# Attention and feed-forward layer on one core: the values matmuls of each step in two halves of 256 queries, with the step loops written out

## What is computed

```python
xn = _layernorm(x)
# attention: 32 query heads of 16, 8 key/value heads, 1024 tokens; bitnet_linear is a matmul with
# the signs of the weights and one factor per output
q, k, v = bitnet_linear(xn, wq, sq), bitnet_linear(xn, wk, sk), bitnet_linear(xn, wv, sv)
scores = jnp.einsum('bhqd,bhkd->bhqk', q, k) / np.sqrt(16)
attn = jax.nn.softmax(scores, axis=-1)
out = jnp.einsum('bhqk,bhkd->bhqd', attn, v)
# feed-forward, 512 -> 1792 -> 512
hidden = _silu(xn @ gate_w.T) * (xn @ up_w.T)
x = x + bitnet_linear(out, wo, so) + hidden @ down_w.T
```

## Time and profile before

| | |
|---|---|
| three runs | 572.05, 576.71, 576.72 us, median 576.71 |
| the profiled execution | 578.11 us |
| its span, first to last instruction | 576.4 us (1.7 us lie around it) |
| PE busy | 513.6 us, 89% |
| DVE busy | 451.4 us, 78% |
| ACT busy | 341.8 us, 59% |
| mean granted TensorE clock | 0.978 |

### The profile page before, as it was taken

One profiled execution on the slowest core, in us unless ns is written; L12 is line 12 of the kernel. 1 busy time (PEld: TensorE's weight loads), 2 busy tenths in 40 slices (PEclk: granted clock), 3 DMA queues, 4 the chain that ended last, 5 costly groups with the idle time before them and its releaser, 6 DMA issues.

```text
span 576.4 us, 9428 instructions
## 1 busy us (share of the span) xinstructions
PE 513.6 (89%) x3001; PEld 162.2 (28%) x3001; DVE 451.4 (78%) x534; ACT 341.8 (59%) x620; POOL 91.0 (16%) x112
## 2 busy tenths in 40 slices
PE   1598977699997999997999997999999998999995
PEld 0354433233332222221222221222222222222442
DVE  6949848776775899997999997999999962221797
ACT  1563324223235788886888886888888875666000
POOL 4503243333323000000000000000001011051021
PEclk9999999899998899998999998999999998999999
DMA  8612654422104421101102102101111003352311
GB/s 251 164 30 63 144 88 92 117 39 37 20 1 58 73 54 37 52 22 36 46 27 54 34 19 56 35 19 54 35 53 58 20 11 89 79 150 66 101 73 55
DMA packets 29949, 36.19 MB, mean 63 GB/s; under 512 B 6544, under 2 KB 20752, under 8 KB 29912
## 3 DMA queue, kind: packets, MB, share of 16 engines
q1 hardware_dynamic: 20600, 24.19, 14.2%
q0 software_dynamic: 8304, 10.95, 10.2%
q10 hardware_dynamic: 1008, 0.61, 0.5%
HBM read 30.62 MB, written 10.35 MB: 71 GB/s over the span
## 4 chain that ended last, share of the span: by engine, by line
PE 71%; DVE 13%; ACT 6%; issue 5%; DMA 2%; ACTq 1%; POOL 0%; SPq 0%; DVEq 0%; POOLq 0%
PE ps L1147 21%; PE ps L1117 16%; PE ps L1033 14%; PE ps L1085 8%; PE ps L1042 7%; ACT room L635 5%; DVE nmx L769 2%; PE ps L1171 2%; PE ps L1014 2%; DVE room L706 1%; DMA ga<-r_scratch 1%; DMA hlo<-x 1%; DVE ga L762 1%; DVE y L765 1%; ACTq L631 1%
## 5 line engine op out<-in xcount | busy, mean ns | idle before, releaser
L769 DVE TENSOR_REDUCE nmx<-ps 128x1 f32<-128x1024 f32 x256 | 302.2, 1219 | 19.1 <-PE ps L1042 14.4
L635 ACT ACTIVATE room<-ps 128x512 f32<-128x512 f32 x512 | 266.3, 604 | 72.3 <-PE ps L1117 67.6
L1117 PE MATMUL ps<-qst,kB 50*128 50x512 f16 x512 | 156.9, 391 | 24.0 <-ACT room L635 16.1
L1042 PE MATMUL ps<-kA,qst 48*128 48x512 f16 x512 | 161.9, 392 | 3.4 <-DVE nmx L769 3.3
L1147 PE MATMUL ps<-room,vcur 128*32 128x512 f32 x1024 | 140.6, 622 | 0.5 <-ACT room L635 0.5
L1033 PE MATMUL ps<-room,wf 128*128 128x512 f16 x448 | 105.2, 390 | 8.3 <-DVE room L864 7.2
L1117 PEld LDWEIGHTS ps<-qst,kB 50*128 50x128 f16 x512 | 37.5, 94 | 178.9 <-ACT room L635 142.2
L1033 PEld LDWEIGHTS ps<-room,wf 128*128 128x128 f16 x448 | 43.3, 100 | 67.6 <-issue 22.4
L616 ACT ACTIVATE room<-ps,gsc 128x512 f32<-128x512 f32 x28 | 19.2, 686 | 68.6 <-PE ps L1033 68.6
L1042 PEld LDWEIGHTS ps<-kA,qst 48*128 48x128 f16 x512 | 35.1, 94 | 43.5 <-DVE nmx L769 35.0
L496 POOL TENSOR_TENSOR hlo<-room,hhi 128x512 f16<-128x512 f32 x28 | 33.5, 1196 | 82.3 <-ACT hhi L573 72.9
(11 more groups left out here) (126 smaller groups left out, 292.9 us busy)
## 6 DMA issues: line engine op xcount, KB each, us to landing
qst<-q_scratch SPq DMA_DIRECT2D x32, 192.0 KB, 3.3
o_scratch<-osb SPq DMA_DIRECT2D x16, 256.0 KB, 2.1
q_scratch<-parts SPq DMA_DIRECT2D x12, 256.0 KB
hlo<-x SPq DMA_DIRECT2D x8, 256.0 KB, 6.8
parts<-x POOLq DMA_DIRECT2D x8, 256.0 KB, 3.2
wf<-gate POOLq DMA_DIRECT2D x14, 128.0 KB, 3.1
wf<-up POOLq DMA_DIRECT2D x14, 128.0 KB, 3.2
wd<-down POOLq DMA_DIRECT2D x1, 1792.0 KB, 13.4
```

Source lines behind the costliest of these rows:

```text
L635: nc.scalar.activation(probs[:, s % 2, r, :], ps[:, score_bank(entry(j, i)), :], ACT.Exp, scale=gam_reg[r]).then_inc(scores_free, 1)
L769: nc.vector.tensor_reduce(nmx[:, hf, idx:idx + 1], bank_pair(idx % 2), AX.X, ALU.max, negate=True).then_inc(rows_free, 1)
L1042: return nc.tensor.matmul(ps[:, 2 * (idx % 2) + b, :], qst[low:low + KROWS, par, hf, head, qt * P:(qt + 1) * P], kA[low:low + KROWS, par, ...
L1117: nc.tensor.matmul(ps[:, score_bank(e), :], kB[low:low + SROWS, par, kt % (TT // 2) * P:(kt % (TT // 2) + 1) * P], qst[low:low + SROWS, pa ...
```

## The change

- The `Fori` loops of all five engines become Python loops: every step is written out.
- `times_values` is issued in two parts of 256 queries: part 0 behind the second score, part 1 behind the fourth. Each has its own four matmuls.
- The four row matmuls of a step follow the first, the second and, two of them, the third score. None follows the fourth.
- `split_max` leaves DVE. ACT copies the transposed maxima to a new tile `mxs` (`take_max`), and POOL makes the two parts from it. PE waits for ACT's copy (`max_taken`) only. POOL's copy of the next group's values (`next_values`) is put between these. `normalize_io(pool, 0)` goes ahead of the last of them.
- ACT loads the next group's factors one in each of the last four steps of a group, into a second set of registers.

```diff
-            def split_max(v, hf, first=False):
-
-                maxT = ps[0:UNITS, 6 if first else score_bank(T_ENTRY), 0:P]
-                dve.wait_ge(maxT_ready, v + 1)
-                nc.vector.tensor_scalar(shp[:, hf, 0, :], maxT, 1.0 / LIFT, None, ALU.mult).then_inc(shift_step, 1)
...
+            def take_max(v, bank):
+
+                act.wait_ge(maxT_ready, v + 1)
+                act.wait_ge(shift_ready, v)
+                nc.scalar.activation(mxs[:, :], ps[0:UNITS, bank, 0:P], ACT.Copy, scale=1.0 / LIFT).then_inc(max_taken, 1)
...
+            def split_max(v, hf):
+
+                pool.wait_ge(max_taken, v + 1)
+                nc.gpsimd.tensor_tensor(shp[:, hf, 0, :], mxs[:, :], ones[0:UNITS, :], ALU.mult).then_inc(shift_step, 1)
+                pool.wait_ge(shift_step, v + 1)
+                nc.gpsimd.tensor_tensor(shp[:, hf, 1, :], mxs[:, :], shp[:, hf, 0, :], ALU.subtract).then_inc(shift_ready, 1)
...
-            with act.Fori(0, NP - 1) as gp:
+            for gp in range(NP - 1):
...
-            def exps(gp, s):
+            def exps(gp, s, last):
...
-                if j == 0 and hf == 0:
-                    for r in range(REP):
-                        act.reg_load(gam_reg[r], gam_words[0:1, bass.ds(gp_ * (2 * REP) + par * REP + r, 1)])
+                if j == T_STEP + 1 and not (last and s >= STEPS + TT):
+                    take_max(gp * 4 + s // TT + 1, score_bank(T_ENTRY))
...
+                if hf == 1 and j >= TT - REP and not (last and par == 1):
+                    load_scale(gp_ * 2 + par + 1, 1 - par, j - (TT - REP))
...
                     if e - 3 == T_ENTRY and transposes:
-                        pe.wait_ge(shift_ready, block_ + 2)
+                        pe.wait_ge(max_taken, block_ + 2)
...
-                    if with_rows:
-                        idx = 2 * j + i // 2
-                        n = (gp_ * 2 + par + 1) * (2 * UNITS) + hf * UNITS + idx
+                    idx = 2 * j + i // 2
+                    if with_rows and i < REP - 1:
                         if i % 2 == 0:
-                            pe.wait_ge(rows_free, n + 1)
+                            pe.wait_ge(rows_free, (gp_ * 2 + par + 1) * (2 * UNITS) + hf * UNITS + idx + 1)
                         mm = half_rows(1 - par, hf, idx, 1 - half)
                         if i % 2 == 1:
                             mm.then_inc(rows_ready, 1)
-                    elif i == 0:
+                        if i == REP - 2:
+                            half_rows(1 - par, hf, idx, half).then_inc(rows_ready, 1)
+                    elif not with_rows and i == 0:
                         for n in fill:
                             down_proj(*FILLS[n])
-                    if i == REP - 1 and not opening:
-                        times_values(gp, s - 1)
+                    if i % 2 == 1 and not opening:
+                        times_values(gp, s - 1, i // 2)
...
+                of = slice(part * (HALF // 2), (part + 1) * (HALF // 2))
                 for r in range(REP):
-                    mm = nc.tensor.matmul(ps[32 * r:32 * r + 32, 7, :], vcur[:, par, key_tile(r, j), :], probs[:, s % 2, r, :],
-                                          start=(j == 0), stop=(j == TT - 1))
-                mm.then_inc(probs_free, 1)
+                    mm = nc.tensor.matmul(ps[32 * r:32 * r + 32, 7, of], vcur[:, par, key_tile(r, j), :],
+                                          probs[:, s % 2, r, of], start=(j == 0 and part == 0),
+                                          stop=(j == TT - 1 and part == 1))
+                if part == 1:
+                    mm.then_inc(probs_free, 1)
```

More of the change, by code:

```diff
@@ L285, in layer_kernel @@
         maxT_ready = sem("maxT_ready")
+        max_taken = sem("max_taken")
         shift_step = sem("shift_step")
@@ L430, in _ @@
             load_shift(1, 0, 1)
-            with sp.Fori(0, NP - 1) as gp:
+            for gp in range(NP - 1):
                 for s in range(TT, 2 * STEPS + 1, TT):
@@ L499, in _ @@
             magnitudes(omags, 1)
+            def split_max(v, hf):
[3 more added lines that the diff above has]
+                nc.gpsimd.tensor_tensor(shp[:, hf, 1, :], mxs[:, :], shp[:, hf, 0, :], ALU.subtract).then_inc(shift_ready, 1)
             for w in range(FU):
                 f, hf = w // 2, w % 2
+                if w == T_AT + 1:
+                    split_max(0, 0)
                 if hf == 0 and 1 <= f <= FT - WF_BUFS:
@@ L511, in _, with next_values @@
             pool.wait_ge(vext_ready, 1)
-            for g in range(2):
-                nc.gpsimd.tensor_copy(vcur[:, g, :, :], vext[:, :, g, :]).then_inc(vcur_ready, 1)
-            with pool.Fori(1, NP) as gp:
-                for par in range(2):
-                    g = gp * 2 + par
-                    pool.wait_ge(probs_free, 2 + STEPS * (g - 1))
-                    nc.gpsimd.tensor_copy(vcur[:, par, :, :],
-                                          vext[:, :, bass.ds(g, 1), :].rearrange("p k g d -> p k (g d)")).then_inc(vcur_ready, 1)
-            for u in range(QT - 1):
+            nc.gpsimd.tensor_copy(vcur[:, 0, :, :], vext[:, :, 0, :]).then_inc(vcur_ready, 1)
+            def next_values(g, par):
+                pool.wait_ge(probs_free, 2 + STEPS * g)
+                nc.gpsimd.tensor_copy(vcur[:, 1 - par, :, :],
+                                      vext[:, :, bass.ds(g + 1, 1), :].rearrange("p k g d -> p k (g d)")).then_inc(vcur_ready, 1)
+            for gp in range(NP - 1):
+                for par in range(2):
+                    split_max(gp * 4 + par * 2 + 1, 1)
+                    next_values(gp * 2 + par, par)
+                    split_max(gp * 4 + par * 2 + 2, 0)
+            split_max(2 * NG - 3, 1)
+            next_values(NG - 2, 0)
+            split_max(2 * NG - 2, 0)
+            normalize_io(pool, 0)
+            split_max(2 * NG - 1, 1)
+            for u in range(1, QT - 1):
                 normalize_io(pool, u)
@@ L608, in _ @@
                                          scale=rescale(n)).then_inc(hi_ready, 1)
+                elif kind == "T":
+                    take_max(0, 6)
                 elif kind == "F":
@@ L653, in _ @@
             act.wait_ge(gam_ready, 1)
-            exps(0, 0)
-            with act.Fori(0, NP - 1) as gp:
+            for r in range(REP):
+                load_scale(0, 0, r)
+            exps(0, 0, False)
+            for gp in range(NP - 1):
                 for s in range(1, 2 * STEPS + 1):
-                    exps(gp, s)
+                    exps(gp, s, False)
                     if s % TT == 0:
@@ L661, in _ @@
                 if s < 2 * STEPS:
-                    exps(NP - 1, s)
+                    exps(NP - 1, s, True)
                 if s % TT == 0:
@@ L875, in _ @@
                     row_max(n, n // UNITS, n % UNITS)
-                elif kind == "T":
-                    split_max(0, 0, True)
             def step_rows(gp, s, last):
@@ L883, in step_rows @@
                 ga_ = gp_ * 2 + par + 1
-                if j == T_STEP + 1 and not (last and s >= STEPS + TT):
-                    split_max(gp * 4 + s // TT + 1, 1 - hf)
                 if with_rows:
@@ L926, in _ @@
             step_rows(0, 0, False)
-            with dve.Fori(0, NP - 1) as gp:
+            for gp in range(NP - 1):
                 for s in range(1, 2 * STEPS + 1):
@@ L1153, in _ @@
             scores(0, 0, False, opening=True)
-            with pe.Fori(0, NP - 1) as gp:
+            for gp in range(NP - 1):
                 for s in range(2 * STEPS):
@@ L1158, in _ @@
                 scores(NP - 1, s + 1, True)
-            times_values(NP - 1, 2 * STEPS - 1)
+            for part in range(2):
+                times_values(NP - 1, 2 * STEPS - 1, part)
             def out_proj(i):
```

29 lines of the change are left out of this document (15 added, 14 removed), and 2 rows, old and new, of the table dve_order.

## The result

| | before | changed |
|---|---|---|
| runs, median | 574.38 us (four; 571.79 to 576.72) | 544.35 us (four; 544.02 to 546.27) |
| profiled execution | 578.11 us | 544.02 us |
| its span | 576.4 us | 542.3 us |
| mean granted clock | 0.978 | 0.987 |

The ratio is 0.9485, with a 95% interval of 0.9425 to 0.9545: faster, by 30.0 us in the medians, against a forecast of 24.1. One more execution of the kernel before was timed beside the changed one, so its median is 574.38 here and 576.71 in the table ahead of the prediction. The prediction took 552.6 us as likeliest and 544 to 558 as its range: 544.35 lies inside, but at the very edge.

What follows compares the result with a forecast made beforehand. A ring of waits, with no engine full, bound ordinary steps; PE bound the last group. Terms -6.4, -10.6, -5.4, -0.3, -1.0, -4.1, +3.7 sum to -24.1: 578.1 to 554.0 profiled, 552.6 us median; range 544 to 558, up to 568 with rivals.

Steps and rivals of the forecast that it cites:

- The ring: Ordinary step before: first exponential, fourth score, values, next first score and exponential wait in turn, setting 2.39 us.
- Rivals A: Ordinary step stays at 2.39 us, through another ring or dearer drains; 565 us in all, chance 0.13.
- B: Ordinary step: fourth score waits for its exponential, making PE's step 2.45 us; 572 us in all, chance 0.06.
- What takes its place: Ordinary step after the change: DVE's two reductions bind at 2.28 us, PE's 2.23 just under.
- The price of a half visit: Values on PE at half the columns: 0.24 us for a round, 0.33 for the last.
- Rival C: Value matmuls on PE: halving the columns does not halve a round; up to 600 us in all, chance 0.05.
- The drain at a change of mode: PE around values: switching tiling mode drains it, 0.10 us in and 0.12 out; last-group step 3.71 us.
- The ordinary step's term, -10.6: Ordinary steps of the 12 blocks: 2.39 to 2.28 us, 0.11 less in 96 steps, -10.6 us.
- Between blocks: -5.4: Block ends: split_max leaves DVE, so 0.45 us is lost instead of 0.9, 12 times, -5.4 us.
- Loops, -6.4: Two blocks with loop jumps: writing loops out removes the stall and slow clock behind it, -6.4 us.
- First and last transposition: PE's waits there for DVE's split: -1.0 us at the first, -4.1 at the last, slow clock included.
- Before the first copy: Opening before 205.39: PE sets the pace at half clock, so the split costs +1.0 us in some three steps.

Runs made afterwards that it cites:

- e3: Changed kernel with the values in one piece behind the fourth score in all steps: 563.80 us, ratio 0.9803.
- e9: Kernel before with loops written out and the split of the maxima on ACT and POOL; values whole, rows in old places: 564.68 us, ratio 0.9829.
- e6: Changed kernel with each row matmul behind its own score again, the last behind the fourth: 544.50 us, ratio 0.9449.
- e5: Changed kernel with the split of the maxima back on DVE, the first transposition's included: 552.03 us, ratio 0.9588.
- e7: Changed kernel with both halves of the values behind the fourth score, one right after the other, in the last group: 542.69 us, ratio 0.9420.
- e4: Changed kernel with the values whole behind the fourth score in the last group alone: 541.31 us, ratio 0.9405.
- e10: e9 with the loops of PE, ACT and DVE back: 565.71 us, ratio 0.9830.
- e1: Kernel before with its five loops written out and nothing else: 570.38 us, ratio 0.9906.
- e12: Changed kernel with values whole in the last group and each block's first step, last-group scores paired and two ACT/DVE output splits a step later: 539.47 us, ratio 0.9376.
- e2: Changed kernel with the loops of PE, ACT and DVE back: 558.51 us, ratio 0.9714.

## Why the prediction was right, and where it was off

The prediction was right in its mechanism and in the direction. Its size came inside the range by little, and several of its terms were made up otherwise than it said.

**The ring: right.** The prediction read 2.39 us as exponential, fourth score, values, first score. e3 keeps everything but the halves and stays on that ring, and so does e9 against e6. PE's step with halves was to be 2.23 us and is 2.22. Rivals A (the step stays at 2.39) and B (the fourth score waits) are out by the rows from 225.49 to 226.83.

**What takes its place: nearly.** DVE's reductions were to bind, with PE just under them. DVE has no gap inside a block, but PE never waits for it there; the step is PE's own 2.22 us. DVE has 0.27 us left in a block, so a little more work on it is felt (e5).

**The price of a half visit: right.** 0.24 for a round and 0.33 for the last one, 0.57 in all: rows 226.03 to 226.60 show the 0.57, not its two parts. Rival C, a round that does not shrink, is out, and e7 shows why with more force: twice the instructions cost nothing. The rule of the Trainium skill on weight loads (TensorE: Matmul & The Clock Gate, Part 3, The mechanism) would have made the loads of these tiles, all of 128 rows, show between rounds; e7's 1.00 us leaves no room for it.

**The drain at a change of mode: right.** The Trainium skill's rule (TensorEngine Tiling (Array Packing), Tiling Modes, Key Properties) and the 0.10 and 0.12 us read from before gave 3.71 us for a step of the last group; it is 3.72. It is the one part of the change that costs, and e4 takes it back.

**The ordinary step's term, -10.6: short by size.** The step went to 2.22 and not to 2.28. Over 96 steps that is 16.3 us, 5.8 more. The term took the longer of the two engines' counts for the step; but PE has room to run ahead of DVE within a block. DVE's 1.14 us was also read from a single pair of reductions. Sixteen in a row are 1.13 apart, a floor of 2.26.

**"Between blocks: -5.4": right for the loops, not what happened here.** The term took the 0.9 us that a block loses beside its steps and gave half of it to the split of the maxima leaving DVE. With the loops in place that comes out: blocks without a jump are 20.07 us on average before and 19.6 in e10, where the split is gone (and with it the old loads of factors; the two were not parted). In straight code it does not: e1 and e9 have the same blocks of 20.01, and lose 0.33 us in each, with DVE's 0.55 us and without. In the changed kernel a block loses 0.6 us beside PE's steps, 0.39 for the copy and 0.21 for the transposition. The prediction named both, with 0.3 and 0.15. A block was to be 8 x 2.28 + 0.45 = 18.69 us and is 8 x 2.22 + 0.61 = 18.37: the step's term was too cautious by 0.48 and the block end's too hopeful by 0.16, which makes 3.8 us in 12 blocks.

**Loops, -6.4: right in the blocks, by luck beside them.** The two jumps' blocks are now like all others. The prediction weighed whether straight code could be short of instructions, and compared the written-out block 432.63 to 452.65 (20.02) with one in the loop (20.08). The two are alike by chance: the written-out steps are longer (2.46 us against 2.39) and the loss beside them is smaller. e10 against e9 shows the 0.4 us a block that this hid. It would have cost 5 us if the ring had stayed, and costs nothing here.

**First and last transposition.** The first: PE's next feed-forward unit starts 0.51 us behind the row matmuls that follow the transposition (137.72 less 137.21) instead of 1.45; -0.9, forecast -1.0. The last and the last group together: 57.4 us from 440.40 to 497.83, against 57.7 from 474.26 to 531.93; -0.2, forecast -0.4. This sum is right by two misses that cancel: the last transposition gives 2.9 us and not 4.1 (these two blocks in e1 and e9: 57.3 and 54.4), and the halves cost 3.0 in them and not 3.7.

**Before the first copy, apart from the first transposition: +1.0 forecast for the slow clock, -3.0 measured, and 2.4 more from nothing in the change.** The stretch with the clock at half was 10.3 us long there before, and is 6.8 us now. The changed kernel's row of busy time by stretches (the granted clock is the column after POOL):

```profile
176.40:183.40 7.00, 5.14 (x28) 1.10 (x30) 3.05 (x3) 5.50 (x10) 1.72 (x3) 0.51 0.74 105
183.40:436.00 252.60, 248.19 (x2654) 62.82 (x2650) 250.10 (x220) 242.64 (x468) 15.75 (x37) 1.00 0.18 46
```

Whether the change shortened the stretch, or only where it happened to begin, was not tried. It was 6.8 us in all other written-out kernels here but two, where it was 3.4 (e6 and e7). The clock then stays full for 252 us, where before it fell to 0.50 behind a jump (270.8 to 274.2) and to 0.51 behind the late split (482.4 to 485.8). The 2.4 us lie ahead of anything that the change touches: 0.7 are there by the feed-forward unit at 95 us (95.47 against 96.21), and 1.7 come where an earlier stretch at half clock falls on matmuls or on a wait. The 3.0 aren't firm either: with the values halved, the first copy falls anywhere from 197.86 (e4) to 201.68 (e12). Part of the difference between the profiled executions is thus chance, and the medians, 30.0 apart, are the better measure. Of the 5.9 us beyond the forecast, 3.8 are the blocks; the rest lies, as far as the traces tell, in the opening, and its cause stays open.

## What to carry to other kernels

Follow a ring of waits through the engines before believing a busy share: VectorE looked full at 2.39 us a step, but its starts alternated, 1.25 and 1.14, and the shorter of the two was its true price. A long visit to one kind of work between two producers can be cut in halves for the price of the changes of mode alone; do it where the ring binds, and not where TensorE is full. When one engine gets faster, look again at each instruction in the others' fixed order that waits for a DMA, and at the length of a loop's body.

## What the runs showed of the hardware

- Sixteen float32 value matmuls of 256 columns, four at a time in groups of 32 columns of the array, take 1.00 us, as eight of 512 do (e7, e4). A change between the row-paired mode and the four-column mode costs 0.10 us going in and 0.12 to 0.14 coming out.
- A taken jump of a loop left ACT without instructions for 2.1 to 2.4 us (before, e10). PE's branch took 0.22 to 0.24 us with a body of some 1,270 recorded instructions (e10), and 5.5 to 5.6 us with some 1,790 (e2).
- An exponential that waits for two semaphores starts 0.49 us behind the matmul that it waits for; where one of the waits is an instruction of its own in its queue (e9), and 0.42 us behind it in a loop, where it is not (before, e10). The kernel before shows 0.49 in its written-out steps. That the separate wait is the cause was not tried by itself.
- DVE's maximum over 128x1024 float32 from PSUM is recorded with 1.22 us, but starts every 1.13 us back to back.
